# Building a row table batch by batch on three engines, with x in the accumulator and the bias in the matrix multiply

## The chip, the cores and the metric

The kernel runs on one core of one Trainium2 chip. The metric is the device time of that core in microseconds (us), the median of three runs. Engines are named as in the profile: PE (TensorE matmul, with PEld for its weight loads), DVE (VectorE), ACT (ScalarE), POOL (GpSimd) and SP (SyncE, which here only issues DMAs).

## The reference

A relational graph layer and then a mixture of experts, both added to x, on 3125 nodes of 256 numbers, 53125 edges (sorted by dst) of 8 relations:

```python
h_all = einsum('ni,roi->rno', layernorm(x), weight)       # 8 relations
messages = segment_sum(h_all[edge_types, src], dst, 3125)
x = x + messages + bias
# then, on layernorm(x): 16 experts of width 512, the best 2 for each node,
# x = x + sum over the two of gate * (silu(n @ w1) * (n @ w2)) @ w3
```

## The kernel before

**Head.** The nodes are 25 tiles of 125 rows, and x comes in five loads of five tiles (`LOAD`, `X_LOADS`). From x the kernel makes a table in HBM, `x_tab`: each normalized row, scaled, is kept as two f16 numbers per element, a high part and a low part (the rest). The stages for this are:

- SP queues three loads of edges (dst, type, src), the ten pieces of x (L386, two for each load), three small tensors, the last of them `gb_sb`, and the relation weights `w_raw`.
- DVE casts the edges (L771 to L773), takes the least and the greatest dst of each chunk of 125 edges (L775, L776), and takes bn_stats of each x tile as its load lands (L782). Only when all 25 are there does it combine them (L784 to L790), for all tiles at once; ACT takes one square root (L594), DVE one reciprocal (L803).
- Then, tile by tile, DVE normalizes (`normalize`, L812) into a ring `xn` of six places, ACT casts to the high part (L600), and DVE subtracts for the low part (L824). For the last five tiles POOL subtracts (L492). SP stores five tiles at a time into `x_tab` (L400).
- POOL, ahead of this, waits for the last x load and for the small tensors, and then adds x and the bias, broadcast to all partitions, into the accumulator `acc` with one instruction over all 25 tiles (L485).
- PE transposes the edge rows and the chunk ends (L1212, L1214) into PSUM, and three eighths of the weights (L1221).
- After the last low part DVE reads the transposed keys (L828) and chunk ends (L830), and works out from them, in some twenty small steps on one partition, the places at which sums are added (L834 to L860). PE spreads a line of them over the partitions (L1228), DVE ends that part at L870 (`edges_done`), and ACT and DVE finish the weights (L610, L877).

**Sweep.** 25 turns follow, one for each node tile. In a turn POOL gathers 17 chunks of 125 rows of `x_tab` (L501, one indirect DMA for each chunk) into `got`, DVE makes one-hot matrices (L882), PE multiplies them in six groups (L1244, `window`), and DVE adds each group into `store` (L900) and then copies that group's indices for the next turn (L902). It is this copy that lets POOL gather the same group of the next turn. The first copy for turn 1 comes after the first add. At the end of a turn ACT takes the sums as a high part (L636) and DVE as a low part (L912), and PE multiplies both with the relation weights in 48 matmuls (L1256, `messages`). DVE adds the result to `acc` (L921), and takes the statistics of the second layernorm. PE's order in turn i is: windows 3, 4, 5 of tile i, transpose, window 0 of tile i+1, gate logits, messages of tile i-1, windows 1 and 2 of tile i+1.

**After the sweep** come routing, the expert loop and the combination of each node's two expert rows with `acc`.

The edges here allow one single sweep; a general form with many sweeps is in the same loops (`tiles_n`, `wins_n`), and its registers are read from counts at run time.

Of the kernel before, what the change touches and what calls it, by code (L numbers as in the profile page):

```python
# [29 lines left out]
I32 = mybir.dt.int32  # L30
ALU = mybir.AluOpType
# [15 lines left out]
POOL_ROWS = LOAD  # L47
# [43 lines left out]
def build(nc, x, src, dst, etype, w_rel, b_rel, gate_w, gate_b, w1, w2, w3, out):  # L91
# [5 lines left out]
    with ExitStack() as ctx:  # L97
# [58 lines left out]
        single_i = sb("single_i", [1, 1], I32)  # L156
        n_tiles = sb("n_tiles", [1, 1], I32)
# [101 lines left out]
        edges_turned = sem("edges_turned")  # L259
        first_ready = sem("first_ready")  # L260
# [11 lines left out]
        pool_low = sem("pool_low")  # L272
# [36 lines left out]
        choice_begun = sem("choice_begun")  # L309
# [14 lines left out]
        half_begun = sem("half_begun")  # L324
# [11 lines left out]
        xs_drained = sem("xs_drained")  # L336
# [34 lines left out]

        def node_tile(i, b, single):
# [6 lines left out]
        def _(sp):  # L379
            for hbm, rows in ((dst, e_dst), (etype, e_typ), (src, e_src)):  # L380
                sp.dma_start(rows, hbm.rearrange("(q e) -> q e", q=EQ)).then_inc(edges_in, 16)
            for n in range(X_LOADS):
                t0, t1 = n * LOAD, (n + 1) * LOAD
                rows = x[t0 * TP:t1 * TP, :].rearrange("(t p) d -> p t d", p=TP)
                for p0, p1 in SPREAD:
                    sp.dma_start(x_sb[p0:p1, t0:t1, :], rows[p0:p1, :, :]).then_inc(x_in[n], 16)  # L386
            sp.dma_start(bias[:, :], b_rel.rearrange("(a d) -> a d", a=1).to_broadcast([P, DIM])).then_inc(small_in, 16)
            sp.dma_start(gw_sb[:, :, :], gate_w.rearrange("(k p) e -> p k e", p=P)).then_inc(small_in, 16)
            sp.dma_start(gb_sb[:, :], gate_b.rearrange("(a d) -> a d", a=1).to_broadcast([P, EXPERTS])).then_inc(small_in, 16)
            sp.dma_start(w_raw, w_rel.rearrange("r (a p) i -> p (r a) i", p=P)).then_inc(w_in, 16)  # L390

            for n in range(X_LOADS):
                sp.wait_ge(row_high, (n + 1) * LOAD)
                sp.wait_ge(row_low, min((n + 1) * LOAD, TILES - POOL_ROWS))
                if (n + 1) * LOAD > TILES - POOL_ROWS:
                    sp.wait_ge(pool_low, (n + 1) * LOAD - (TILES - POOL_ROWS))
# [28 lines left out]
            for n in range(X_LOADS):  # L425
                t0, t1 = n * LOAD, (n + 1) * LOAD
                sp.wait_ge(x2_kept, before + (t1 + 1))
                sp.sem_inc(half_begun, 1)
# [7 lines left out]
            def store_oct(q):  # L436
                for n in range(2):
                    sp.wait_ge(oct_got[n], (q + 1) * HALF_OCT * 16)
                    sp.sem_inc(half_begun, 1)
# [3 lines left out]
                    sp.sem_inc(half_begun, 1)  # L443
# [24 lines left out]
        def _(pool):  # L468
# [12 lines left out]
            nc.gpsimd.memset(logit[:, :, :], 0.0).then_inc(acc_init, 1)  # L481
            for n in range(X_LOADS):
                pool.wait_ge(x_in[n], 2 * 16)
            pool.wait_ge(small_in, 48)
# [4 lines left out]
            for t in range(TILES - POOL_ROWS, TILES):  # L489
                pool.wait_ge(row_high, t + 1)  # L490
                row = got[0:TP, t % (3 * LOAD), :]
                nc.gpsimd.tensor_tensor(row[:, DIM:], xn[0:TP, t % XN, :], row[:, 0:DIM], ALU.subtract).then_inc(pool_low, 1)  # L492
# [95 lines left out]
        def _(act):  # L588
# [849 lines left out]
```

## Time and profile before

| | |
|---|---|
| median of three runs | 1097.66 us (1096.2 to 1099.3) |
| time of the profiled execution | 1098.44 us |
| its span, first to last instruction | 1096.7 us |
| busy: PE, POOL, DVE, ACT | 761.1, 730.0, 613.2, 331.7 us |
| granted PE clock, mean share of full speed | 0.828 |

The profile is of one execution. Busy time is a sum over the span, and says little of which engine sets the end of a stage. The time of the profiled execution is that of the same run from outside, 1.7 us more than its span. In a row of a timeline the first number is the start, the second how long the instruction, or the merged run of `xN` instructions, took; in brackets stands how long the engine sat idle before, and what ended that.

### The profile page before, as it was taken

To read this page: it belongs to the slowest core of one execution; us is meant where nothing else is said; L and a number is where in the kernel's file an instruction comes from. 1 tells how busy PE (TensorE), PEld (TensorE's weight loads), DVE (VectorE), ACT (ScalarE), POOL (GpSimd) and SP (SyncE) were. 2 spreads that over 40 slices of the span, in tenths; PEclk is the share of its full clock that TensorE was granted. 3 is DMA by queue.
4 is the path that set the end of the run, shared out by engine and by line. 5 is a ranking of instruction groups with operands and counts; after the bars stand their busy time and mean duration, and the time that the engine had idled before them with its cause. 6 is when DMAs were issued, how large, how long until landed. Compare 5 with 4: busy or idle time off the path is not lost.

```text
span 1096.7 us, 18853 instructions
## 1 busy us (share of the span) xinstructions
PE 761.1 (69%) x4904; PEld 651.1 (59%) x4905; DVE 613.2 (56%) x1431; ACT 331.7 (30%) x368; POOL 730.0 (67%) x627
## 2 busy tenths in 40 slices
PE   1137668767688767887767863289999899997600
PEld 1024557756577655676656752278887788886500
DVE  5975575656746566665665767854443334433433
ACT  0332333335433344333453343122322223221100
POOL 2467777777777777777777720667363777767476
PEclk9656887988877898788887886599999989998855
DMA  9253454444544333433334314077355357555346
GB/s 212 75 184 100 135 159 133 129 129 129 158 120 122 96 96 100 119 96 100 97 96 121 95 41 139 29 230 239 115 177 172 97 189 236 161 191 112 91 125 179
DMA packets 93628, 145.97 MB, mean 133 GB/s; under 512 B 13367, under 2 KB 67595, under 8 KB 93610
## 3 DMA queue, kind: packets, MB, share of 16 engines
q0 software_dynamic: 25968, 70.94, 23.2%
q1 hardware_dynamic: 50794, 59.48, 17.2%
q10 hardware_dynamic: 16848, 15.34, 4.5%
q8 instruction: 7, 0.11, 0.0%
q14 instruction: 11, 0.09, 0.0%
HBM read 109.90 MB, written 33.98 MB: 131 GB/s over the span
## 4 chain that ended last, share of the span: by engine, by line
PE 37%; issue 17%; DMA 14%; POOL 13%; DVE 9%; ACT 4%; DVEq 3%; SPq 1%; ACTq 1%; POOLq 0%
PE ps L1256 12%; PE ps L1378 9%; POOL got L501 7%; PE ps L1244 7%; PE ps L1360 6%; DMA got<-x_tab,idx 5%; DMA y_tab<-ffn 5%; ACT part L636 3%; POOL x_sb L571 2%; POOL store L582 2%; PE ps L1386 1%; DMA xs_tab<-x_sb 1%; DVE store L900 1%; DVE mean L784 1%; DVEq L900 1%
## 5 line engine op out<-in xcount | busy, mean ns | idle before, releaser
L501 POOL DMA_INDIRECT got<-x_tab,idx x425 | 446.5, 1051 | 134.3 <-issue 112.7
L1244 PE MATMUL ps<-hot,got 125*128 125x256 f16 x1700 | 252.3, 312 | 140.2 <-DMA got<-x_tab,idx 126.1
L1244 PEld LDWEIGHTS ps<-hot,got 125*128 125x128 f16 x1700 | 178.8, 110 | 202.1 <-issue 139.6
L1378 PE MATMUL ps<-part,operands 128*128 x696 | 177.9, 405 | 1.2 <-DVE operands L1133 1.2
L900 DVE TENSOR_TENSOR store<-store,ps 128x512 f32 x150 | 102.7, 685 | 136.0 <-PE ps L1244 126.9
L1256 PE MATMUL ps<-part 128*128 128x256 f32 x1152 | 166.7, 312 | 1.0 <-DVE part L912 0.8
L1256 PEld LDWEIGHTS ps<-part 128*128 128x128 f32 x1152 | 163.0, 221 | 1.6 <-DVE part L912 1.3
L1378 PEld LDWEIGHTS ps<-part,operands 128*128 128x128 f32 x696 | 129.3, 192 | 27.0 <-issue 2.0
L912 DVE SCALAR_TENSOR_TENSOR part<-store,part 128x1024 fp32r<-128x1024 f32 x48 | 94.8, 2019 | 64.9 <-ACT part L636 64.9
L882 DVE TENSOR_SCALAR hot<-key_row,pass,drel 125x256 f16<-125x256 f16 x425 | 126.2, 367 | 5.7 <-issue 5.1
L1360 PE MATMUL ps<-part,operands 128*128 x696 | 101.7, 296 | 24.3 <-DVE operands L1143 24.1
L636 ACT ACTIVATE part<-store 128x2048 fp32r x24 | 93.8, 3906 | 48.8 <-DVE store L900 48.8
L1360 PEld LDWEIGHTS ps<-part,operands 128*128 128x128 f32 x696 | 90.1, 195 | 30.1 <-issue 28.2
L621 ACT ACTIVATE dev<-mv,eps 125x1 f32<-125x1 f32 x25 | 7.4, 295 | 317.5 <-DVE mv L927 317.5
L524 POOL TENSOR_TENSOR part<-store,part 128x2048 fp32r<-128x2048 f32 (+1 forms) x28 | 97.9, 3496 | 2.3
L1143 DVE TENSOR_TENSOR operands<-ps,operands 128x512 fp32r<-128x512 f32 x58 | 40.1, 691 | 95.5 <-ACT operands L701 95.5
L701 ACT CAST operands<-ps 128x512 fp32r<-128x512 f32 x58 | 34.1, 587 | 181.7 <-issue 90.0
L522 POOL TENSOR_SCALAR part<-store 128x2048 fp32r<-128x2048 f32 (+1 forms) x28 | 41.6, 1486 | 70.6 <-PE ps L1378 58.3
L535 POOL DMA_INDIRECT x_sb<-x_tab,oct_idx x64 | 61.0, 954 | 23.4 <-issue 16.2
L1139 DVE COPY ffn<-ps 128x256 f32<-128x256 f32 x58 | 24.6, 425 | 66.9 <-PE ps L1360 43.3
L1153 DVE TENSOR_TENSOR ffn<-ffn,ps 128x512 f32<-128x512 f32 x58 | 39.7, 685 | 32.5 <-PE ps L1378 25.5
L643 ACT COPY store<-store x25 | 56.2, 2246 | 0.0
(200 smaller groups left out, 700.6 us busy)
## 6 DMA issues: line engine op xcount, KB each, us to landing
store<-in_L_ffn_w SPq DMA_DIRECT2D x48, 512.0 KB, 5.8
xs_tab<-x_sb SPq DMA_DIRECT2D x16, 512.0 KB, 3.5
y_tab<-ffn SPq DMA_DIRECT2D x9, 896.0 KB
ffn<-xs_tab ACTq DMA_DIRECT2D x59, 128.0 KB, 2.2
y_tab<-ffn ACTq DMA_DIRECT2D x58, 128.0 KB
got<-x_tab,idx POOLq DMA_INDIRECT x425, 2.8
x_sb<-in_x SPq DMA_DIRECT2D x5, 560.0 KB
x_tab<-got SPq DMA_DIRECT2D x5, 560.0 KB
```

What stands on the lines that cost most here:

```text
L501: nc.gpsimd.indirect_dma_start(got[:, c, :], None, x_tab, bass.IndirectOffsetOnAxis(ap=idx[:, c:c + 1], axis=0)).then_inc(gathered[c], 16)
L524: nc.gpsimd.tensor_tensor(part[:, 2 * k + 1, at:at + cols], whole, high.bitcast(F32), ALU.subtract).then_inc(done, 1)
L535: nc.gpsimd.indirect_dma_start(xg[:, u, :], None, x2_tab, bass.IndirectOffsetOnAxis(ap=oct_idx[:, u:u + 1], axis=0)).then_inc(oct_got[u // ...
L636: nc.scalar.activation(high, buffer(v, 0, P * RELS).rearrange("p k (n r) -> p k r n", r=RELS), ACT.Copy, scale=1.0 / SCALE).then_inc(tile_ ...
L643: nc.scalar.copy(buffer(v + 1, 0, BK - TK), buffer(v, TK, BK)).then_inc(moved_on, 1)
L882: v.tensor_scalar(hot[0:CE, g % HOT, c - GROUPS[g][0], :], key_row[0:CE, :], pass0[0:CE, 0:1], drel[0:CE, bass.ds(turn * TC + c, 1)], ALU. ...
L900: v.tensor_tensor(window, window, ps[:, WIN_BANK[g], :].rearrange("p (k n) -> p k n", k=KT), ALU.add).then_inc(win_added, 1)
L912: last = v.scalar_tensor_tensor(out=low[:, k, :, :], in0=whole_sums, scalar=1.0 / SCALE, in1=high[:, k, :, :].bitcast(F32), op0=ALU.mult, ...
L1244: last = mm(ps[:, WIN_BANK[g], k * KEYS:(k + 1) * KEYS], got[0:CE, c, a * DIM + k * P:a * DIM + (k + 1) * P], hot[0:CE, g % HOT, c - c0, : ...
L1256: last = mm(ps[:, bank, 0:DIM], (high, low)[a][:, k, r, :], wT[:, b, k, r * DIM:(r + 1) * DIM], start=(r == 0 and k == 0 and a + b == 0), ...
L1360: last = mm(ps[:, Y_BANK, 0:DIM], hidT[:, a, k, :], part3[:, bass.ds(at + b, 1), k, :].rearrange("p a n -> p (a n)"), start=(k == 0 and a ...
L1378: last = mm(ps[:, UP_BANK + w, :], xsT[:, a, k, :], part12[:, bass.ds(at + b, 1), w, k, :].rearrange("p a n -> p (a n)"), start=(k == 0 an ...
```

## The change

- **Loads.** x goes straight into `acc`. SP issues loads 0, 2 and 4, ACT issues 1 and 3. The bias is one row of 1 KB and stands beside a row of zeros (`bias[1, 2, DIM]`).
- **Statistics.** For each load DVE takes bn_stats and then bn_aggr tile by tile, ACT one square root, DVE one reciprocal (`statistics`, `spread_x`).
- **Rows.** POOL normalizes all 25 tiles, ACT casts, DVE subtracts all 25 (`low_rows`). DVE's order is statistics of batch n, then low rows of batch n-1; ACT's is the root of batch n+1, then the casts of batch n.
- **Edges.** The least and greatest dst of the chunks are taken after the last low row. Their ten transposes move in PE's order behind the first three eighths of the weights and have a semaphore of their own (`ends_turned`), which DVE awaits behind the copy of the keys.
- **Bias.** POOL's large add is gone. `messages` starts with one f32 matmul, a column of ones against one row of `bias`: the bias at a tile's first visit, the zeros at any later one. PE chooses the row by a register.
- Some semaphores of no effect on the order are merged (`half_begun`, `choice_begun`, `xs_drained`).

```diff
@@ sync
-            for n in range(X_LOADS):
...
-                    sp.dma_start(x_sb[p0:p1, t0:t1, :], rows[p0:p1, :, :]).then_inc(x_in[n], 16)
-            sp.dma_start(bias[:, :], b_rel.rearrange("(a d) -> a d", a=1).to_broadcast([P, DIM])).then_inc(small_in, 16)
+            for n in range(0, X_LOADS, 2):
                 for p0, p1 in SPREAD:
+                    sp.dma_start(acc[p0:p1, n * LOAD:(n + 1) * LOAD, :], x_rows(n)[p0:p1, :, :]).then_inc(x_in[n], 16)
...
+            sp.dma_start(bias[:, 0, :], b_rel.rearrange("(a d) -> a d", a=1)).then_inc(small_in, 16)
...
-                sp.wait_ge(row_high, (n + 1) * LOAD)
-                sp.wait_ge(row_low, min((n + 1) * LOAD, TILES - POOL_ROWS))
...
+                sp.wait_ge(row_low, (n + 1) * LOAD)
@@ gpsimd
-            nc.gpsimd.tensor_tensor(acc[:, :, :], x_sb[0:TP, :, :], bc(bias[0:TP, :], [TP, TILES, DIM], 1),
-                                    ALU.add).then_inc(acc_init, 1)
...
+            pool.wait_ge(iota_used, 1)
+            for t in range(TILES):
+                if t % LOAD == 0:
+                    pool.wait_ge(rstd_done, t // LOAD + 1)
+                if t >= XN:
+                    pool.wait_ge(row_low, t - XN + 1)
+                nc.gpsimd.tensor_scalar(xn[0:TP, t % XN, :], acc[:, t, :], mv[0:TP, t, 0:1], rstd[0:TP, t:t + 1],
+                                        ALU.subtract, ALU.mult).then_inc(xn_ready, 1)
@@ scalar
+            for n in range(1, X_LOADS, 2):
+                for p0, p1 in SPREAD:
+                    act.dma_start(acc[p0:p1, n * LOAD:(n + 1) * LOAD, :], x_rows(n)[p0:p1, :, :]).then_inc(x_in[n], 16)
...
+            def spread_x(n):
+                t0, t1 = n * LOAD, (n + 1) * LOAD
+                act.wait_ge(stats_done, t1)
+                nc.scalar.activation(dev[0:TP, t0:t1], mv[0:TP, t0:t1, 1], ACT.Sqrt, bias=eps[0:TP, 1:2], scale=SCALE ** -2).then_inc(dev_done, 1)
+            spread_x(0)
             for t in range(TILES):
+                if t % LOAD == 0 and t + LOAD < TILES:
+                    spread_x(t // LOAD + 1)
                 act.wait_ge(xn_ready, t + 1)
...
@@ vector
+            v.tensor_copy(src_f, e_src).then_inc(edge_rows, 1)
+            def statistics(n):
+                t0, t1 = n * LOAD, (n + 1) * LOAD
+                dve.wait_ge(x_in[n], 2 * 16)
+                for t in range(t0, t1):
+                    v.bn_stats(stat[0:TP, t, :], acc[:, t, :]).then_inc(stats_raw, 1)
+                for t in range(t0, t1):
+                    dve.wait_ge(stats_raw, t + 1)
+                    v.bn_aggr(mv[0:TP, t, :], stat[0:TP, t, :]).then_inc(stats_done, 1)
+                dve.wait_ge(dev_done, n + 1)
+                v.reciprocal(rstd[0:TP, t0:t1], dev[0:TP, t0:t1]).then_inc(rstd_done, 1)
+            def low_rows(n):
+                for t in range(n * LOAD, (n + 1) * LOAD):
+                    dve.wait_ge(row_high, t + 1)
+                    row = got[0:TP, t % (3 * LOAD), :]
+                    v.tensor_tensor(row[:, DIM:], xn[0:TP, t % XN, :], row[:, 0:DIM], ALU.subtract).then_inc(row_low, 1)
+            statistics(0)
+            for n in range(1, X_LOADS):
+                statistics(n)
+                low_rows(n - 1)
...
+            low_rows(X_LOADS - 1)
             by_chunk = dst_f.rearrange("p (j e) -> p j e", j=EJ)
             v.tensor_reduce(ends[:, 0, :], by_chunk, AX.X, ALU.min)
+            v.tensor_reduce(ends[:, 1, :], by_chunk, AX.X, ALU.max).then_inc(ends_ready, 1)
...
+            dve.wait_ge(ends_turned, 1)
@@ tensor
+            pe.wait_ge(ends_ready, 1)
+            for j in range(EJ):
+                for n in range(2):
+                    last = nc.tensor.transpose(ps[0:1, 2 + n, j * EQ:(j + 1) * EQ], ends[:, n, j:j + 1], ident[0:EQ, 0:EQ])
+            last.then_inc(ends_turned, 1)
...
+            def messages(v0, i, w, bank=MSG_BANK, high=tileT[:, 0, :, :, :], low=tileT[:, 1, :, :, :]):
+                n = v0 + i
+                pe.reg_alu(bias_row, pe.snap((w + i) * several, min_val=0), 1, ALU.min)
                 pe.wait_ge(tile_low, n + 2)
                 if bank == MSG_BANK:
                     pe.wait_ge(acc_added, n + 1)
+                which = pe.snap(bias_row, min_val=0, max_val=1)
+                mm(ps[:, bank, 0:DIM], ones[0:1, :], bias[0:1, bass.ds(which, 1), :].rearrange("p a d -> p (a d)"), start=True, stop=False)
```

## Rows read from the trace of the kernel before

**Rows 1.** Page, part 5 (groups of instructions): POOL's gathers.

```profile
L501 POOL DMA_INDIRECT got<-x_tab,idx x425 | 446.5, 1051 | 134.3 <-issue 112.7
```

**Rows 2.** Waits of POOL, 84 to 640 us: in total, times, longest.

```profile
POOL got L501 <- issue: 103.0, 338, 0.3
...
POOL got L501 <- DVE idx L902: 21.6, 71, 0.3
```

**Rows 3.** Timeline of POOL: start, duration, instruction, [idle before].

```profile
25.59 13.68 POOL L485 TENSOR_TENSOR acc<-x_sb,bias 125x6400 f32<-125x6400 f32 x1 [20.89 <-DMA gb_sb<-in_L_ffn_gate_b]
...
54.93 3.69 POOL L492 TENSOR_TENSOR got<-hot,got 125x256 f16<-125x256 f32 x5 [15.66 <-ACT got L600]
...
63.73 1.23 POOL L501 DMA_INDIRECT got<-x_tab,idx  x1 [5.11 <-issue]
...
85.36 0.95 POOL L501 DMA_INDIRECT got<-x_tab,idx  x1 [0.30 <-DVE idx L902]
...
638.50 0.94 POOL L501 DMA_INDIRECT got<-x_tab,idx  x1 [0.30 <-issue]
```

**Rows 4.** Timeline of DVE, 0 to 84 us.

```profile
13.09 0.79 DVE L776 TENSOR_REDUCE ends<-store 85x5 f32<-85x625 f32 x1
...
13.86 1.73 DVE L782 BATCH_NORM_STATS2 stat<-x_sb 125x6 f32<-125x256 f32 x5
...
24.83 1.73 DVE L782 BATCH_NORM_STATS2 stat<-x_sb 125x6 f32<-125x256 f32 x5 [1.19 <-DMA x_sb<-in_x]
...
26.60 12.73 DVE L784 TENSOR_TENSOR mean<-stat 125x25 f32<-125x25 f32 x1
...
58.65 0.92 DVE L828 COPY key_c<-ps 125x425 f32<-125x425 f32 x1 [1.22 <-POOL got L492]
...
59.61 1.84 DVE L830 COPY store<-ps 1x425 f32<-1x425 f32 x2
...
83.32 0.41 DVE L902 COPY idx<-gidx 125x3 int32<-125x3 int32 x1
```

**Rows 5.** Windows view: stretch, busy us by engine, PEclk, DMA share, GB/s.

```profile
8.00:10.00 2.00, 0.00 (x0) 0.00 (x0) 0.00 (x0) 0.00 (x0) 0.00 (x0) 1.00 1.11 236
...
64.00:79.00 15.00, 6.31 (x22) 4.42 (x22) 9.76 (x29) 5.63 (x7) 11.37 (x12) 0.50 0.64 219
```

**Rows 6.** Timelines of ACT and DVE: single operations that the change multiplies.

```profile
40.11 0.32 ACT L594 ACTIVATE dev<-var,eps 125x25 f32<-125x25 f32 x1 [37.71 <-DVE var L790]
...
43.26 0.41 ACT L600 CAST got<-hot 125x256 f16<-125x256 f32 x1 [0.25 <-DVE hot L812]
...
54.99 0.42 DVE L824 TENSOR_TENSOR got<-hot,got 125x256 f16<-125x256 f32 x1
...
593.24 0.18 DVE L927 BATCH_NORM_AGGREGATE mv<-stat 125x2 f32<-125x6 f32 x1 [0.15 <-DVE stat L924]
```

**Rows 7.** Groups of POOL by form: the two tensor_scalar sizes.

```profile
L522 POOL TENSOR_SCALAR part<-store 128x2048 fp32r<-128x2048 f32 x14 | 26.8, 1918 | 68.8 <-PE ps L1378 58.3 <-DMA store<-in_L_ffn_w 10.3
...
L522 POOL TENSOR_SCALAR part<-store 128x1024 fp32r<-128x1024 f32 x14 | 14.8, 1055 | 1.7 <-PE ps L1360 1.7
```

**Rows 8.** Timeline of PE, 0 to 90 us.

```profile
14.02 0.69 PE L1212 MATMUL ps<-ident,store 85*125 85x85 f32 x2 [14.02 <-DVE ends L776]
...
17.31 0.49 PE L1214 MATMUL ps<-ident,ends 85*1 85x85 f32 x2
...
65.54 1.78 PE L1228 MATMUL ps<-store,ones 1*128 1x426 f32 x2 [31.77 <-DVE store L849]
...
79.39 8.93 PE L1244 MATMUL ps<-hot,got 125*128 125x256 f16 x68 [5.20 <-DVE hot L882]
```

**Rows 9.** Timelines of PE and DVE around one turn.

```profile
582.11 6.80 PE L1256 MATMUL ps<-part 128*128 128x256 f32 x48
...
602.86 8.19 PE L1256 MATMUL ps<-part 128*128 128x256 f32 x48 [0.41 <-DVE part L912]
...
598.86 3.95 DVE L912 SCALAR_TENSOR_TENSOR part<-store,part 128x1024 fp32r<-128x1024 f32 x2 [2.70 <-ACT part L636]
```

More of the change, by code:

```diff
@@ L480, in _ @@
             nc.gpsimd.memset(ffn[:, :], 0.0).then_inc(zeros_set, 1)
[L481 to L484, printed above, removed]
[L485 to L492 removed]
+            nc.gpsimd.memset(logit[:, :, :], 0.0).then_inc(rows_zeroed, 1)
+            nc.gpsimd.memset(bias[:, 1, :], 0.0).then_inc(rows_zeroed, 1)
+            pool.wait_ge(iota_used, 1)
[6 more added lines that the diff above has]
+                                        ALU.subtract, ALU.mult).then_inc(xn_ready, 1)
             def gather_turn(n):
@@ L774, in _ @@
+            low_rows(X_LOADS - 1)
             by_chunk = dst_f.rearrange("p (j e) -> p j e", j=EJ)
             v.tensor_reduce(ends[:, 0, :], by_chunk, AX.X, ALU.min)
-            v.tensor_reduce(ends[:, 1, :], by_chunk, AX.X, ALU.max).then_inc(edge_rows, 1)
-            for n in range(X_LOADS):
-                dve.wait_ge(x_in[n], 2 * 16)
-                for t in range(n * LOAD, (n + 1) * LOAD):
-                    v.bn_stats(stat[0:TP, t, :], x_sb[0:TP, t, :]).then_inc(stats_raw, 1)
-            dve.wait_ge(stats_raw, TILES)
@@ L784, in _ @@
-            v.tensor_tensor(mean[0:TP, :], stat[0:TP, :, 1], stat[0:TP, :, 4], ALU.add)
-            v.tensor_tensor(var[0:TP, :], stat[0:TP, :, 2], stat[0:TP, :, 5], ALU.add)
-            step(v.tensor_tensor(dev[0:TP, :], stat[0:TP, :, 1], stat[0:TP, :, 4], ALU.subtract))
-            v.tensor_scalar(mean[0:TP, :], mean[0:TP, :], 0.5, None, ALU.mult)
-            step(v.scalar_tensor_tensor(out=dev[0:TP, :], in0=dev[0:TP, :], scalar=0.25, in1=dev[0:TP, :],
-                                        op0=ALU.mult, op1=ALU.mult))
@@ L856, in _ @@
                                    op0=ALU.mult, op1=ALU.add).then_inc(counts_ready, 1)
+            v.tensor_scalar(several_i[:, :], even[:, :], -1.0, 1.0, ALU.mult, ALU.add)
             v.tensor_copy(single_i[:, :], even[:, :]).then_inc(counts_ready, 1)
@@ L1211, in _ @@
                 for bank, rows in ((0, src_f), (1, key_f)):
-                    nc.tensor.transpose(ps[0:CE, bank, out_cols], rows[:, j * CE:(j + 1) * CE], ident[0:EQ, 0:EQ])
-                for n in range(2):
-                    last = nc.tensor.transpose(ps[0:1, 2 + n, out_cols], ends[:, n, j:j + 1], ident[0:EQ, 0:EQ])
+                    last = nc.tensor.transpose(ps[0:CE, bank, out_cols], rows[:, j * CE:(j + 1) * CE], ident[0:EQ, 0:EQ])
             last.then_inc(edges_turned, 1)
@@ L1284, in _ @@
             wins_n = pe.value_load(n_wins[0:1, 0:1], min_val=1, max_val=GEN_W)
+            several = pe.value_load(several_i[0:1, 0:1], min_val=0, max_val=1)
+            pe.wait_ge(small_in, 48)
+            pe.wait_ge(rows_zeroed, 2)
             with pe.Fori(0, tiles_n) as b:
```

89 lines of the change are left out of this document (30 added, 59 removed).

## The prediction

> **What bounds the kernel now.** I read the page first, then the waits of POOL, then the timelines of the first 90 us. The page's largest group is POOL's gather: 425 of them, 446.5 us busy and 134.3 us idle before them, of which 112.7 are a fixed 0.3 us of issue each [rows 1]. In the waits of 84 to 640 us no single wait of POOL lasts over 0.3 us, and the one on DVE's index copy, 71 times, is no longer than the ordinary issue [rows 2]. So in the sweep POOL is never kept waiting: it issues from 63.73 to 638.50 without a gap [rows 3], (638.50 - 63.73) / 424 = 1.356 us for each gather, 23.05 us for a turn of 17. A gather by itself takes 0.95 + 0.30 = 1.25, which makes 21.25 a turn; the missing 1.8 us are gathers that stretch beside L912. **The sweep is a rigid block on POOL. What the head saves or loses is what its first gather, or a gather soon after it, moves.**
>
> The head before: x lands in five loads, the first by 13.86, the last at 24.83 [rows 4]. Then DVE's first two-input operation, 25 numbers wide, takes 12.73 us, from 26.60 to 39.33. A bn_aggr on as little data takes 0.18 [rows 6]. It ends with POOL's add over all tiles, 25.59 + 13.68 = 39.27 [rows 3]: DVE was shut out by it. The last low row is done at 54.93 + 3.69 = 58.62; call this time T. The first gather starts at T + 5.1, after the last table store. On DVE the chain of small steps starts at T too, and ends in the first index copy, at 83.32 + 0.41 = 83.7 = T + 25.1. The eighteenth gather, the first that needs this copy, starts at 85.36 = T + 26.7. So only 1.6 us of slack lie between the DVE chain and POOL's stream.
>
> **The change, step by step.** First T itself.
>
> 1. *First load.* The loads are (24.83 - 13.86) / 4 = 2.74 us apart, with the DMA engines' share already at 1.11 [rows 4, 5]: transfers set the pace, not their issue. ACT now queues loads 1 and 3 at once, beside SP's edges and load 0. If they share the engines, load 0 waits for both: 13.86 + 2 x 2.74 = 19.3. The edges come later too, by 0 to 5.5, with 1.7 us of casts behind them; that is under this wait. Bounds for this step: 13.9 (load 0 undisturbed) and 19.3. I take the late end, since the engines are full. (The Trainium skill, DMA: Bandwidth & Descriptors, section "Issuing engines are not separate DMA queues", says that transfers from several issuing engines interleave on the same sixteen DMA engines, and that spreading saves only issue time. The share in the trace agrees. It speaks against this edit: by it the last load lands no earlier and the first one later. Were it wrong, the second queue would add bandwidth, and the sum below would be 5.5 us smaller, 1083.7.)
> 2. *Statistics of a batch.* Five bn_stats 1.73 [rows 4], five bn_aggr at up to 0.18 alone [rows 6], overlapped about 0.12, so 0.6: 2.3 us. ACT's root 0.32 [rows 6] and two hand-overs of 0.1: 0.5. Reciprocal 0.2. POOL starts on batch 0 at 19.3 + 3.0 = 22.3.
> 3. *A POOL row.* No tensor_scalar of 256 columns with pointer scalars is in the trace. From 2048 and 1024 columns the slope is (1918 - 1055) / 1024 = 0.84 ns a column, the rest 0.19 us, so 0.41 us a row [rows 7]. Above it stands the two-input 3.69 / 5 = 0.74 [rows 3]. I take 0.41, as the rows are of the same operation; five are 2.1 us, which fit beside DVE's next statistics.
> 4. *Low rows of a batch.* ACT casts batch n-1 only after the root of batch n: first cast 0.4 us [rows 6]. DVE then subtracts five times. Alone one takes 0.42, starting every 0.33; POOL is then at batch n, whose rows each wait for a place in the ring that a low row frees. Bounds for a low row: 0.33 and 0.42 + 0.41 = 0.83 if they exclude each other. In the five rows where POOL and DVE alternated before, POOL kept its own pace. I take 0.5, so 2.5 a batch.
> 5. *Sum for T.* 22.3 + 2.8 (statistics 1 and root) + 0.4 + 2.5 + 1.2 (the index casts that stand here once, the first like L828's 0.92) = 29.2. Three cycles of 2.8 + 0.4 + 2.5 = 5.7 make 46.3; five last low rows, with nothing beside them, 1.8. T = 48.1, against 58.6: **-10.5 us**. This is near the 12.5 us for which DVE was shut out; that is the gain, and batching gives back in late load and hand-overs most of what it overlaps.
>
> Now what follows T.
>
> 6. *Table store to first gather.* One store after the last low row as before, T + 5.1: moves with T.
> 7. *Chunk ends.* The two reductions, 0.79 each and slightly overlapped [rows 4], come after T: 1.5 us. Then ten transposes: twenty took 17.31 + 0.49 - 14.02 = 3.8 us [rows 8], so 1.9, and 0.2 for hand-overs: ready at T + 3.6. The key copy (0.92) runs under them. Before, the copies of the ends began at 59.61 = T + 1.0. The chain is 2.6 us longer, 0.1 more for `several_i`, and the index copy comes at T + 27.8, where POOL would want it at T + 26.7: **+1.0 us** of stall, at the first gather of turn 1. Groups behind it have slack: POOL takes 3.8 us for three gathers, DVE's copies come each 1.4.
> 8. *Bias matmul.* The nearest row is the f32 matmul of one row of 426 columns at 1.78 us [rows 8], at a granted clock of 0.50 [rows 5], that is at 1.2 of 2.4 GHz: 1.78 x 256 / 426 = 1.07 at that clock, 0.53 at full. It stands between L912 and the 48 matmuls, on PE's own loop. That loop, from messages to messages without a wait for a gather, is 602.86 - 582.11 = 20.75 us [rows 9] in a turn of 23.05. So 2.3 us a turn cover it, and **0.5** is my allowance for turns in which messages take 8.2 in place of 6.8 us. Without cover it would be 24 x 0.5 to 1.1, 13 to 26 us. At the end of the sweep, with no gathers left, one of the last two is bare: **+0.5**.
> 9. *At nothing:* the x loads' issue on ACT (ACT has nothing to do until the first root), the bias row's load (it is needed 50 us later), PE's extra register load, which runs while PE waits for one-hots until 79.39 [rows 8], the merged semaphores, and the removed add itself, in whose time POOL was idle but for DVE's being shut out. Without their cover the first would cost some 5 us (two loads' share of the issue of five), the register load 0.5, the bias load one short DMA.
>
> Sum: -10.5 + 1.0 + 0.5 + 0.5 = **-8.5 us**. The profiled execution took 1098.44 us, 1.7 more than its span, which I leave alone: 1089.9. It lay 0.8 above the median of the runs, so I predict **1089.2**.
>
> **Rivals.**
> - *POOL and DVE exclude each other in the low rows.* For it: L784. Against: five POOL rows in 3.69 us with DVE working between. At 0.83 a low row four batches take 4 x 1.65 = 6.6 us longer: 1095.8. (The Trainium skill, SBUF — State Buffer, section "Who interferes with whom", has a DVE instruction with two SBUF inputs and a GpSimd instruction that reads SBUF block each other fully. L784 against L485 agrees. By it this would be the likely case, but it tells only that they take turns, not how long POOL's turn is in a short instruction.) Chance 0.12.
> - *Load 0 is not held up,* since SP's entries are ahead in time: T 5.5 earlier, 1083.7. Against: edges and load 0 need the engines long after ACT's first issue. Chance 0.13.
> - *PE becomes the bound of the sweep: slower.* The place is the start of `messages`. If matmul, register work and the waits around it cost more than 2.3 us a turn, all above that is paid 24 times. At 2.8 it is 24 x 0.5 = 12 in place of the 0.5 allowed: 1100.7. The point from which the kernel is slower than before is 2.3 + 9.0 / 24 = 2.7 us. Against: two such matmuls' row says 0.5 to 1.1. Chance 0.06.
> - *The gathers' beat against L912 changes.* 1.8 us are lost each turn there, more or less by phase, and every phase is new: about 0.1 us a turn, +-2.4. This widens the range, with no side.
>
> **How the numbers follow.** The forecast case (a gain of 5 to 12 us) has 0.63, and 1086 to 1093 as its own range; 0.06 are left for what I don't see, half of it on either side of no gain. The 8-in-10 range takes in the second rival and most of the first: 1083 to 1095. A difference of 0.3%, 3.3 us, is about what a measurement of this kernel can tell. Faster by more: 0.63 + 0.13 + a third of the first rival + 0.02 = 0.82. Within it: 0.11. Slower: 0.07.
>
> **What the next profile would show.** Load 0's bn_stats at about 19 and not 14 (step 1); no DVE operation of 12 us; POOL rows of about 0.41 (step 3); cycles of 5.7 us (4); the last low row at 48 (5); first gather 5.1 behind it (6); at the first gather of turn 1 a wait of about 1 us on the index copy (7); one f32 matmul before each `messages`, POOL still without waits until the last gather, and (last - first) / 424 still 1.35 (8). Wrong would make it: POOL rows well above 0.5, which count 25 times in the ring; a wait of POOL on DVE in each turn; or a first gather that no longer follows T by 5.1.

## The result and the profile after

| | before | after |
|---|---|---|
| median of the runs | 1096.93 us (1094.58 to 1099.3) | 1112.78 us (1111.38 to 1115.73) |
| ratio, 95% interval | 1 | 1.0148 (1.0117 to 1.0179) |
| span of the profiled execution | 1096.7 us | 1109.7 us |
| granted PE clock, mean | 0.828 | 0.825 |

Slower by 15.9 us where 8.5 less were forecast. The two spans differ by 13.0 us. I cut both at three events of POOL: the first gather, the last gather, and the first large operation behind the sweep (`x_sb<-got,tile`, L540 before, L535 after).

| | before | after | difference | forecast |
|---|---|---|---|---|
| start to first gather | 63.73 | 59.39 | -4.3 | -10.5 |
| first to last gather (the sweep) | 574.77 | 589.84 | +15.1 | +1.5 |
| last gather to POOL's large operation | 47.88 | 54.39 | +6.5 | +0.5 |
| from there to the end | 410.32 | 406.08 | -4.2 | 0 |

**The head.** Timeline of POOL after, beside [rows 3]:

```profile
21.95 31.48 POOL L486 TENSOR_SCALAR hot<-acc,mv,rstd 125x256 f32<-125x256 f32 x25 [16.83 <-DVE rstd L790]
59.39 1.17 POOL L496 DMA_INDIRECT got<-x_tab,idx  x1 [5.96 <-issue]
...
82.58 0.95 POOL L496 DMA_INDIRECT got<-x_tab,idx  x1 [1.90 <-DVE idx L890]
```

The 25 rows run without a gap, 31.48 us in all, one each 1.26 us, where 0.41 was forecast. A row takes 1.22 us by itself and up to 1.65 where three of DVE's low rows fall into it. Everything else in the head keeps up with them. Timelines of DVE and ACT, beside [rows 4, 6]:

```profile
17.77 1.73 DVE L785 BATCH_NORM_STATS2 stat<-acc 125x6 f32<-125x256 f32 x5 [3.32 <-DMA acc<-in_x]
21.56 0.19 DVE L790 RECIPROCAL rstd<-dev 125x5 f32<-125x5 f32 x1 [1.71 <-ACT dev L597]
...
52.70 0.43 DVE L796 TENSOR_TENSOR got<-hot,got 125x256 f16<-125x256 f32 x1 [0.78 <-ACT got L606]
53.90 0.42 DVE L796 TENSOR_TENSOR got<-hot,got 125x256 f16<-125x256 f32 x1 [0.78 <-ACT got L606]
...
57.48 1.83 DVE L817 COPY store<-ps 1x425 f32<-1x425 f32 x2 [0.91 <-PE ps L1216]
```

```profile
19.93 1.28 ACT L597 ACT_TABLE_LOAD   x1 [19.93 <-DVE mv L788]
21.23 0.30 ACT L597 ACTIVATE dev<-mv,eps 125x5 f32<-125x5 f32 x1
```

DVE waits 0.78 us for each low row. T, the end of the last one, is 53.90 + 0.42 = 54.3. The first gather is 5.06 behind it.

**The sweep.** Waits of POOL, 84 to 649 us, beside [rows 2]:

```profile
POOL got L496 <- issue: 99.7, 327, 0.3
POOL got L496 <- DVE idx L890: 33.8, 79, 1.1
```

POOL now waits for DVE's index copy for up to 1.1 us, which it never did before. The starts of every seventeenth gather give the length of the 24 full turns, 0 to 23: turns 0 to 7 take 21.4 to 23.8 us, and **each of turns 8 to 23 takes 23.87 to 23.92**. Something with a fixed beat of 23.89 has taken over from POOL, whose mean was 23.05. The groups of POOL and PE on the page after show which, beside [rows 1]:

```profile
L496 POOL DMA_INDIRECT got<-x_tab,idx x425 | 450.2, 1059 | 146.5 <-issue 110.8
L1236 PE MATMUL ps<-hot,got 125*128 125x256 f16 x1700 | 204.6, 281 | 32.4 <-DVE hot L870 16.4
...
L1254 PE MATMUL ps<-part 128*128 128x256 f32 x1152 | 205.9, 359 | 0.0
```

The same two groups of PE before:

```profile
L1244 PE MATMUL ps<-hot,got 125*128 125x256 f16 x1700 | 252.3, 312 | 140.2 <-DMA got<-x_tab,idx 126.1
...
L1256 PE MATMUL ps<-part 128*128 128x256 f32 x1152 | 166.7, 312 | 1.0 <-DVE part L912 0.8
```

The windows of PE hardly wait for gathers any more: 32.4 us idle before them in all, against 140.2. The messages, 166.7 us busy and 312 ns each before, take 205.9 and 359. The profile's chain of the work that ended last says the same: in its stretch from 300 to 600 us it holds 76.6 us of POOL's gathers and their DMAs before, and none after. One turn of the timelines of PE, DVE and ACT, beside [rows 9]:

```profile
520.82 8.63 PE L1254 MATMUL ps<-part 128*128 128x256 f32 x48
...
536.92 1.47 PE L1236 MATMUL ps<-hot,got 125*128 125x256 f16 x12 [0.52 <-DVE hot L870]
541.95 1.02 PE L1275 MATMUL ps<-gw_sb,x2T 128*125 128x16 f32 x4 [3.56 <-ACT x2T L635]
543.58 1.21 PE L1250 MATMUL ps<-bias,ones 1*128 x2 [0.61 <-DVE part L900]
544.72 8.62 PE L1254 MATMUL ps<-part 128*128 128x256 f32 x48
```

```profile
534.33 0.69 DVE L888 TENSOR_TENSOR store<-store,ps 128x512 f32 x1 [0.50 <-issue]
...
539.38 3.96 DVE L900 SCALAR_TENSOR_TENSOR part<-store,part 128x1024 fp32r<-128x1024 f32 x2 [2.71 <-ACT part L641]
```

```profile
535.26 3.92 ACT L641 ACTIVATE part<-store 128x2048 fp32r x1 [1.10 <-DVE store L888]
539.08 2.25 ACT L648 COPY store<-store  x1
541.23 0.41 ACT L632 COPY x_sb<-xn 125x256 f32 x1
```

The chain of waits is closed in itself: the last window's sum (L888) frees ACT's split (L641), that frees DVE's (L900), then come the bias matmul, the 48 matmuls, and the windows that stand behind them in PE's order. This is the loop of step 8; I call it PE's ring from here on (it has nothing to do with the ring `xn`). The granted clock in the same turn (windows view; busy us of PE, PEld, DVE, ACT, POOL, then PEclk):

```profile
536.00:538.50 2.50, 1.86 (x14) 1.26 (x14) 0.68 (x3) 2.50 (x1) 1.93 (x2) 1.00 0.36 105
538.50:542.00 3.50, 0.05 (x1) 0.05 (x1) 2.62 (x2) 3.50 (x5) 3.15 (x2) 0.78 0.25 75
542.00:544.70 2.70, 2.09 (x6) 1.36 (x6) 2.70 (x7) 1.66 (x1) 1.81 (x2) 0.50 0.19 49
544.70:549.00 4.30, 4.30 (x21) 4.28 (x21) 4.30 (x17) 0.00 (x0) 3.20 (x4) 0.50 0.31 91
550.00:553.00 3.00, 3.00 (x24) 3.00 (x24) 0.00 (x0) 0.00 (x0) 2.39 (x3) 0.88 0.36 105
553.00:555.00 2.00, 2.00 (x20) 1.78 (x20) 0.00 (x0) 0.00 (x0) 1.39 (x3) 1.00 0.34 105
```

PE stands idle for 3.56 us before the gate logits. In that gap the grant falls from 1.00 to 0.50 of 2.4 GHz, and the bias matmul and the first 6 us of the messages run at 1.2 GHz; the grant is 1.00 again only at 550.8. So messages take 8.6 us, where [rows 9] show 6.80 in the turn from which I took the loop.

That gives a theory in numbers. The loop was 20.75 with messages at 6.80; at the lower clock it is 20.75 + 1.8 = 22.6, still under POOL's 23.05, by 0.5. The bias matmul adds 1.21 and its hand-over 0.1: 23.9, over it. The rows bear this out part by part. One more is needed from DVE's timeline before:

```profile
593.81 0.69 DVE L900 TENSOR_TENSOR store<-store,ps 128x512 f32 x1 [0.38 <-issue]
```

| part of the ring | before, 582.11 to 602.86 | after, 520.82 to 544.72 |
|---|---|---|
| start of the messages to the last window's sum | 11.70 | 13.51 |
| from there to the end of DVE's split | 9.00 | 9.01 |
| end of DVE's split to the next messages | 0.05 | 1.38 |
| sum | 20.75 | 23.90 |

1.8 of the 3.15 us come from the slower messages, 1.3 from the bias matmul.

### The profile page after: what moved, and what is told of

The parts are those of the page before. It is cut to its first block, busy times and chain, and to the rows that moved or that the text cites. A ratio compares the mean times of both kernels' runs of the same rounds, so it can differ in the third digit from the quotient of the medians.

```text
span 1109.7 us, 19013 instructions
## 1 busy us (share of the span) xinstructions
PE 791.8 (71%) x4954; PEld 685.0 (62%) x4955; DVE 595.1 (54%) x1435; ACT 331.8 (30%) x372; POOL 748.0 (67%) x647
## 4 chain that ended last, share of the span: by engine, by line
PE 42%; issue 16%; DVE 11%; POOL 10%; ACT 8%; DMA 8%; DVEq 3%; ACTq 1%; POOLq 0%; SPq 0%
PE ps L1254 17%; PE ps L1379 10%; ACT part L641 8%; PE ps L1361 6%; DVE part L900 4%; PE ps L1236 4%; DMA y_tab<-ffn 3%; POOL hot L486 3%; PE ps L1250 2%; POOL x_sb L566 2%; DVE store L888 2%; POOL store L577 2%; PE ps L1387 2%; DMA acc<-in_x 1%; POOL got L496 1%
## 5 line engine op out<-in xcount | busy, mean ns | idle before, releaser
L1236 PE MATMUL ps<-hot,got 125*128 125x256 f16 x1700 | 204.6, 281 | 32.4 <-DVE hot L870 16.4
L1254 PEld LDWEIGHTS ps<-part 128*128 128x128 f32 x1152 | 201.0, 270 | 15.6 <-issue 15.6
L1254 PE MATMUL ps<-part 128*128 128x256 f32 x1152 | 205.9, 359 | 0.0
L1236 PEld LDWEIGHTS ps<-hot,got 125*128 125x128 f16 x1700 | 166.6, 100 | 63.4 <-issue 34.9
L888 DVE TENSOR_TENSOR store<-store,ps 128x512 f32 x150 | 103.1, 687 | 158.9 <-PE ps L1236 146.3
L900 DVE SCALAR_TENSOR_TENSOR part<-store,part 128x1024 fp32r<-128x1024 f32 x48 | 94.8, 2019 | 66.0 <-ACT part L641 66.0
L870 DVE TENSOR_SCALAR hot<-key_row,pass,drel 125x256 f16<-125x256 f16 x425 | 123.1, 357 | 4.8 <-issue 4.8
L641 ACT ACTIVATE part<-store 128x2048 fp32r x24 | 93.9, 3912 | 50.6 <-DVE store L888 50.6
L1275 PE MATMUL ps<-gw_sb,x2T 128*125 128x16 f32 x100 | 24.7, 366 | 78.6 <-ACT x2T L635 78.6
L1275 PEld LDWEIGHTS ps<-gw_sb,x2T 128*125 128x125 f32 x100 | 22.1, 310 | 85.7 <-ACT x2T L635 85.7
```

Of the source, the lines that this page charges most:

```text
L641: nc.scalar.activation(high, buffer(v, 0, P * RELS).rearrange("p k (n r) -> p k r n", r=RELS), ACT.Copy, scale=1.0 / SCALE).then_inc(tile_ ...
L870: v.tensor_scalar(hot[0:CE, g % HOT, c - GROUPS[g][0], :], key_row[0:CE, :], pass0[0:CE, 0:1], drel[0:CE, bass.ds(turn * TC + c, 1)], ALU. ...
L888: v.tensor_tensor(window, window, ps[:, WIN_BANK[g], :].rearrange("p (k n) -> p k n", k=KT), ALU.add).then_inc(win_added, 1)
L900: last = v.scalar_tensor_tensor(out=low[:, k, :, :], in0=whole_sums, scalar=1.0 / SCALE, in1=high[:, k, :, :].bitcast(F32), op0=ALU.mult, ...
L1236: last = mm(ps[:, WIN_BANK[g], k * KEYS:(k + 1) * KEYS], got[0:CE, c, a * DIM + k * P:a * DIM + (k + 1) * P], hot[0:CE, g % HOT, c - c0, : ...
L1254: last = mm(ps[:, bank, 0:DIM], (high, low)[a][:, k, r, :], wT[:, b, k, r * DIM:(r + 1) * DIM], start=False, stop=(r == RELS - 1 and k == ...
```

## The experiments

Twelve kernels. Unless said otherwise a kernel is the one after with the edit shown. The phases are those of the table above, from one profiled execution each; "msgs" is the mean time of the 24 groups of 48 matmuls in us, "ratio" is the time against the kernel before on the same chip, with its 95% interval.

| | first gather | sweep | to POOL's large op. | rest | msgs | ratio |
|---|---|---|---|---|---|---|
| before | 63.7 | 574.8 | 47.9 | 410.3 | 6.95 | 1 |
| after | 59.4 | 589.8 | 54.4 | 406.1 | 8.58 | 1.0148 |
| no_bias_matmul | 60.2 | 572.7 | 50.3 | 399.4 | 6.78 | 0.9892 (0.9863 to 0.9920) |
| before_plus_zero_row | 64.5 | 587.8 | 54.6 | 409.6 | 8.56 | 1.0192 (1.0165 to 1.0219) |
| bias_in_the_gap | 60.3 | 575.4 | 54.3 | 404.8 | 7.85 | 1.0005 (0.9980 to 1.0031) |
| rows_with_constants | 57.3 | 587.9 | 54.4 | 399.6 | 8.22 | 1.0020 (0.9997 to 1.0043) |
| gap_filled | 60.5 | 576.7 | 50.2 | 403.9 | 6.18 | 0.9978 (0.9951 to 1.0006) |
| bias_f16_pair | 58.3 | 575.6 | 50.4 | 406.1 | 7.84 | 0.9993 (0.9970 to 1.0017) |
| rows_mult_add | 51.6 | 588.2 | 54.4 | 397.7 | 8.52 | 0.9973 (0.9952 to 0.9993) |
| split_rows_early_bias | 54.2 | 577.1 | 54.0 | 406.6 | 7.89 | 0.9964 (0.9951 to 0.9978) |
| all_three_small | 49.5 | 573.5 | 53.0 | 406.8 | 7.85 | 0.9915 (0.9890 to 0.9941) |
| all_three_and_filler | 50.3 | 574.4 | 51.1 | 406.6 | 6.15 | 0.9908 (0.9882 to 0.9934) |
| before_gap_filled | 64.9 | 572.2 | 53.1 | 412.9 | 6.07 | 1.0073 (1.0050 to 1.0096) |

The column "rest" falls into three sets: 409.6 to 412.9 for the three kernels made from before, 403.9 to 406.8 for the seven made from after whose values are the full ones, 397.7 to 399.6 for the three that change values. The last three change the numbers on which the experts are chosen, so some 7 us of their gain need not be the edit's, and I read them by their other columns.

**no_bias_matmul**: without the bias matmul and its register (the bias is left out of the sum; the first of the 48 matmuls now starts it).

```diff
-                which = pe.snap(bias_row, min_val=0, max_val=1)
-                mm(ps[:, bank, 0:DIM], ones[0:1, :], bias[0:1, bass.ds(which, 1), :]..., start=True, stop=False)
```

> The changed kernel without its bias matmul and without the register work before it, so the bias is left out of the result. Theory A (the bias matmul stands on PE's own loop and makes that loop, not POOL, the bound of the sweep): from the first gather to the last, 589.8 us in the changed kernel, comes back to 575 to 578; POOL's wait on the index copy goes from most turns; the time falls from 1112.8 to about 1092 (the head's 4.3 us gain stays). Rival B (the new head or other placement sets the gathers' beat; the matmul is covered): the sweep stays near 590 us and the time near 1111.

Measured: no beat of 23.9, turns of 22.5 to 23.7 from turn 2 on, the sweep 17.2 us shorter than after's and 2.1 shorter than before's. The whole loss in the sweep comes with the bias matmul and its register work, though the matmul is only 1.21 us long; bias_f16_pair, below, keeps the register work and has no beat either.

**before_plus_zero_row**: the kernel before with the same matmul, a row of zeros, in front of its messages.

> The kernel before, with a matmul of a row of zeros at the head of each group of messages, chosen by the same register work; nothing else. Theory A: the sweep goes from 574.8 to about 590 us, turns lock to 23.9 us, the time to 1112 to 1118. Rival B: the sweep stays within 3 us of 574.8, and the time within 4 us of 1097.

```profile
POOL got L505 <- issue: 98.8, 324, 0.3
POOL got L505 <- DVE idx L907: 32.7, 77, 1.1
```

Waits of its POOL: the picture of after, though head and x's path are the old ones. Each turn from 8 to 23 takes 23.84 to 23.98 us, and +13.0 us of sweep and +6.7 behind it follow. The loss doesn't depend on the rest of the change.

**bias_in_the_gap**: the matmul and its waits stand ahead of the gate logits, where PE has its idle gap in the kernel after (and likewise at the end of the sweep).

```diff
                         window(v0, i + 1, 0)
+                        bias_first(v0, i - 1, w)
                         if norm:
                             gate_logits(v0 + i - 2)
```

> The changed kernel with the bias matmul moved ahead of the gate logits, where PE sits idle for 3.6 us in each turn. Theory A1 (the matmul's own 1.2 to 1.5 us on the loop is what costs): a turn falls from 23.9 to at most 22.9, POOL is the bound again, and the time is 1092 to 1096. Theory A2 (the larger part is that PE falls to the lower clock in that gap and does all the messages at 1.2 GHz, 8.6 us against 6.9 on average before): the messages still take 8.6 us; the turn is near 22.7 with POOL again ahead, since a small matmul doesn't keep the clock up. If neither holds (B), the time stays at 1111.

```profile
531.00 1.22 PE L1248 MATMUL ps<-bias,ones 1*128 x2
532.15 1.02 PE L1280 MATMUL ps<-gw_sb,x2T 128*125 128x16 f32 x4
533.01 8.02 PE L1259 MATMUL ps<-part 128*128 128x256 f32 x48
```

The same matmul at the same 1.2 us, no longer behind DVE's split: sweep 575.4, no fixed beat, though the messages take 7.85 us on the mean and nearly all begin at a grant of 0.50. It is the place in the ring that costs, not PE's added work. What stays is the stretch behind the last gather, 54.3 as in after; I come back to it.

**gap_filled**: the bias matmul stays, and twelve more f32 matmuls of the identity, whose results nobody uses, go ahead of the gate logits.

```diff
                         window(v0, i + 1, 0)
                         if norm:
+                            pe.wait_ge(acc_added, v0 + i)
+                            for _ in range(12):
+                                mm(ps[:, MSG_BANK, DIM:DIM + P], ident[:, :], ident[:, :], start=True, stop=True)
                             gate_logits(v0 + i - 2)
```

> The changed kernel, the bias matmul at its place, with twelve f32 matmuls of 128 columns (2.7 us, results unused) put into PE's idle gap of 3.6 us ahead of the gate logits. They take nothing off the loop. Theory A2 (PE falls to 1.2 GHz in that gap and does the messages there, 8.6 us): the granted clock at the start of the messages is 1.0 in place of 0.5, the messages take 6.0 to 6.9 us, a turn comes back to about 23.0 with POOL the bound, and the time falls from 1112.8 to 1090 to 1098. Theory A1 (only the bias matmul's own time counts): messages stay at 8.6 and the turn at 23.9 or more, the time at 1112 or above.

Timeline of its PE, and its clock in the windows view:

```profile
530.63 3.04 PE L1305 MATMUL ps<-ident 128*128 128x128 f32 x24
533.51 0.51 PE L1275 MATMUL ps<-gw_sb,x2T 128*125 128x16 f32 x4
533.95 0.69 PE L1250 MATMUL ps<-bias,ones 1*128 x2
534.57 6.01 PE L1254 MATMUL ps<-part 128*128 128x256 f32 x48
```

```profile
532.00:538.00 6.00, 6.00 (x50) 5.64 (x49) 6.00 (x20) 1.10 (x1) 4.78 (x5) 1.00 0.31 87
```

The grant stays at 1.00. The filler costs 3.0 us, and gate logits (1.02 to 0.51), bias (1.21 to 0.69) and messages (8.62 to 6.01) give back 3.6: the kernel is 18 us faster than after with more work in it. The filler was meant to end ahead of L900's end. In the trace it doesn't: in this turn L900 ends at 532.80 and the filler 0.9 us later, and in 20 of the 22 turns that have it the filler ends 0.7 to 3.1 us behind L900, in the other two later still. PE comes late there because POOL is the bound again and the window ahead waits for a gather (2.26 us in this turn). So the run shows that at the higher clock the ring fits under POOL's turn even with the filler; that a ring-bound turn would hide the filler in its gap is argued, not shown.

**bias_f16_pair**: the matmul at its old place, but cheap: the bias as high and low f16 rows, one pass each.

```diff
-                mm(ps[:, bank, 0:DIM], ones[0:1, :], bias[0:1, bass.ds(which, 1), :]..., start=True, stop=False)
+                for part_n in range(2):
+                    mm(ps[:, bank, 0:DIM], ones_h[:, :], bias_h[:, bass.ds(which * ((2 - part_n) * DIM) + part_n * DIM, DIM)], start=(part_n == 0), stop=False)
```

> The changed kernel with the bias as two f16 rows (high and low part), so two one-pass matmuls of 256 columns at the same place in place of one f32 matmul of 1.2 us: about 0.45 us at 1.2 GHz. Both theories of the loop: 0.8 us less than 23.9 leaves 23.1 a turn, just at POOL's own pace of 23.0, so the lock is loose; sweep 575 to 580 us, time 1094 to 1102. If the register work and the waits, not the matmul's passes, make the 1.2 us, the turn stays at 23.7 or more and the time at 1108 or above.

The bias row now comes over ACT's queue, ACT makes its high part and POOL its low part, all ahead of the statistics. The pair takes 0.60 us. By the sum above the ring is 22.6 + 0.6 = 23.2, next to POOL's 23.05. Measured: turns of up to 23.7 but no beat, POOL's longest wait on the index copy 0.3 us again, sweep 575.6. So the point of decision lies between 0.6 and 1.2 us of added matmul, not at the 2.7 of the forecast. The head gained by a side effect. ACT's copy for the high part brings its table loads forward:

```profile
5.39 1.28 ACT L598 ACT_TABLE_LOAD   x1 [5.39 <-DVEq L777]
...
7.11 1.28 ACT L604 ACT_TABLE_LOAD   x1
```

The first reciprocal comes 2.4 us behind the first bn_stats, not 3.8. The three kernels below that use the pair have this too.

**rows_with_constants** and **rows_mult_add**: where do POOL's 1.2 us come from? The first puts constants in place of the per-row mean and rstd and keeps subtract and multiply (the rows aren't normalized); the second multiplies by a constant and adds 0.

```diff
-                nc.gpsimd.tensor_scalar(..., mv[0:TP, t, 0:1], rstd[0:TP, t:t + 1], ALU.subtract, ALU.mult)
+                nc.gpsimd.tensor_scalar(..., 0.0, SCALE, ALU.subtract, ALU.mult)      # rows_with_constants
+                nc.gpsimd.tensor_scalar(..., SCALE, 0.0, ALU.mult, ALU.add)           # rows_mult_add
```

> The changed kernel with POOL's normalization by constants (0 and 2048) in place of each row's own mean and root; all waits stay. Theory P (the two scalars read from SBUF for each partition make POOL's operation slow, 1.21 us): a row takes 0.4 to 0.5 us, the last low row is done 5 to 6 us earlier than at 54.3, and the time falls to about 1107. Rival S (a short f32 operation on POOL costs 1.2 whatever its scalars, or DVE's subtract shuts it out): the row stays at 1.1 to 1.2 us and the time at 1112.

> The changed kernel with POOL's row operation as times 2048 plus 0 (the form of operation of POOL's weight splits) in place of minus 0 times 2048, which took 1.07 us. Theory O (subtract is what POOL is slow at): a row takes 0.4 to 0.5 us, the last low row is done near 49. Rival F (an operation of 256 columns costs POOL 1.07 us whatever it is, the straight line from 1024 and 2048 columns being wrong for short ones): 1.07 stays and the last low row at 52.2. The time is 1096 to 1107 either way, as the sweep may fall into its 23.9 us pattern early or late.

Timeline of POOL in rows_mult_add:

```profile
22.51 5.27 POOL L486 TENSOR_SCALAR hot<-acc 125x256 f32<-125x256 f32 x10 [17.39 <-DVE rstd L790]
```

With constants a row takes 1.07 us, so the pointers are worth 0.15. With multiply and add it takes 0.41 by itself and 0.46 to 0.52, once 0.69, beside DVE's low rows, and T comes down to 46.3. The price hangs on the pair of operations. L522 of [rows 7], from which the 0.41 was extrapolated, multiplies and adds. The head gained 7.8 us over after's, and the sweep's beat of 23.9 came all the same (from turn 9; with constants from turn 10).

**split_rows_early_bias**: DVE normalizes the first two rows of each batch, POOL three; f16 pair, placed in the gap.

> A version meant to beat both: the f16 bias pair moved into PE's gap ahead of the gate logits, and DVE normalizes the first two rows of each batch of five, POOL the other three (3.6 us of POOL for each cycle of DVE of about 5.5). Theory: POOL's 25 x 1.2 us no longer set the head; the last low row is done at 46 to 49 in place of 54.3, the first gather 5 later; the sweep is POOL's at 573 to 576 us; the time is 1080 to 1088. If DVE and POOL hold each other up in the rows, the last low row stays above 51 and the time is 1088 to 1093.

T 49.1, sweep 577.1: the first version with the full values that is faster than both. The last three rows still wait for POOL at 1.2 us each.

**all_three_small** and **all_three_and_filler**: real rows as multiply and add, f16 pair, in the gap; the second with ten filler matmuls ahead of the pair.

```diff
+                dve.wait_ge(rstd_done, n * 2 + 1)
+                v.scalar_tensor_tensor(mv[0:TP, t0:t1, 0], mv[0:TP, t0:t1, 0], -1.0, rstd[0:TP, t0:t1], ALU.mult, ALU.mult).then_inc(rstd_done, 1)
...
-                nc.gpsimd.tensor_scalar(..., mv[0:TP, t, 0:1], rstd[0:TP, t:t + 1], ALU.subtract, ALU.mult)
+                nc.gpsimd.tensor_scalar(..., rstd[0:TP, t:t + 1], mv[0:TP, t, 0:1], ALU.mult, ALU.add)
```

> The kernel after with three edits: the POOL row as x times rstd plus minus mean times rstd (multiply, add, with pointer scalars), one more small DVE operation per batch for the second scalar; the bias as two one-pass f16 rows; and this pair placed ahead of the gate logits. Theory O (the pair of operations sets the row's price, 0.41 to 0.46 with constants): rows 0.45 to 0.6 us with pointers, T about 47, first gather about 52. Theory S (the loop of the PE is the bound only where its turn exceeds 23.1 us): no lock, sweep 573 to 577 as in bias_in_the_gap and bias_f16_pair. Together 1096.6 - 12 to - 7 = about 1085 to 1090. Rival P (a gain at the head is given back, since the turns of the sweep take what the PE and DVE allow): sweep 580 or more and 1093.

> all_three_small plus ten f32 128-column matmuls of ident in the PE's gap ahead of the bias pair and the gate logits. If the clock of the messages matters although the loop is not the bound (PE less behind at the end of the sweep): messages 6.0 to 6.5 us, the stretch from the last gather to the first POOL add 47 to 50 us instead of 52 to 54, time 2 to 5 us below all_three_small, about 1083. If only the lock matters: the same time within 1 us.

Timeline of POOL in all_three_small:

```profile
20.96 6.58 POOL L490 TENSOR_SCALAR hot<-acc,rstd,mv 125x256 f32<-125x256 f32 x10 [13.24 <-DVE mv L799]
29.86 3.73 POOL L490 TENSOR_SCALAR hot<-acc,rstd,mv 125x256 f32<-125x256 f32 x5 [2.31 <-DVE mv L799]
34.48 3.73 POOL L490 TENSOR_SCALAR hot<-acc,rstd,mv 125x256 f32<-125x256 f32 x5 [0.89 <-DVE mv L799]
39.09 4.39 POOL L490 TENSOR_SCALAR hot<-acc,rstd,mv 125x256 f32<-125x256 f32 x5 [0.89 <-DVE mv L799]
```

These are merged runs of five or ten rows. A single row with pointers takes 0.55 us by itself; beside two or three of DVE's low rows it takes 0.97 to 1.22, which happens twice in each batch but the first and lifts the mean to 0.75. POOL waits for DVE between the batches, and T is 44.4, under the 48.1 of the forecast; some 1.3 us of this is ACT's table load, off the path as in bias_f16_pair. 1086.79 us against 1097.84: this is the gain that the change could have had. The filler on top gives nothing that can be told (1085.66, the intervals overlap): messages come down from 7.85 to 6.15 and the stretch behind the last gather by 1.9, but sweep and head are 0.8 or 0.9 longer in that profile.

**before_gap_filled**: the filler of twelve in the kernel before.

> The kernel before with twelve f32 128-column matmuls of ident ahead of the gate logits of each turn. The turn of before is set by POOL (23.05 us on the mean), so that a higher clock of the messages (6.9 to about 6.2 us) buys nothing in the turns: theory S says 1095 to 1098, within 0.3%. If the clock sets the time of before also: 1085 to 1090.

Missed on the bad side: 1105.02 us, 1.0073 times before. Messages did fall from 6.95 to 6.07, and the sweep only from 574.8 to 572.2, as POOL sets it. But the stretch behind the last gather grew by 5.2. I read this as PE, with 3 us more work in each turn, being further behind POOL when the gathers end; no run separates it. The same filler gave 18 us in after and costs 8 here. Another 2.6 us are lost behind POOL's large operation and 1.2 ahead of the first gather, where this kernel has no edit; what makes them is open.

**before_merged_semaphores**: only the merge of the counters, for the 5 us in "rest".

> The kernel before with only the merge of the counters that nothing waits for (the old half_begun, choice_begun and xs_drained now counted in tiles_begun and stats2_begun), which the prediction costed at nothing. Open point: from POOL's large add to the end the three kernels made from before took 409.6 to 412.9 us, the seven made from after with all values kept 403.9 to 406.8, some 5 us less. If the merge makes this: 404 to 407 us there, and a time 0.4% below before. If not (other addresses or another phase): 409 to 413 us and the same time within 0.3%, sweep and head as before. I expect the second.

It ran on another chip, on which the kernel before took 1311.05 us as well; the ratio is 0.9995 (0.9983 to 1.0007). The merge does nothing there. Its profile can't be set against the others' by phases, so that what shortens the rest by some 5 us in the kernels made from after stays open.

## Why the prediction was wrong, step by step

Between the forecast and the spans lie 21.5 us: 6.2 in the head, 13.6 in the sweep, 6.0 behind its last gather, and 4.2 the other way in the rest, for which nothing was forecast.

**Step 8 failed, and it turned the change into a loss.** With the same matmul off the ring (bias_in_the_gap) the time is that of before, 1.0005. The step took "a loop of 20.75 in a turn of 23.05, so 2.3 us cover it". The size of the matmul was nearly right (1.07 forecast at the low clock, 1.21 measured). The slack was wrong: 20.75 came from one turn whose messages took 6.80, while the row of the very next turn showed 8.19. At the low clock the ring is 22.6 and the cover 0.5. I saw the 8.19 and paid it with an allowance of 0.5 us for the whole sweep, as if it only came now and then. It was common: before, the grant in the first microsecond of the messages was under 0.6 in 18 of 24 turns, and messages took 6.00 to 8.50 us as it came back sooner or later. (The turn of the 20.75 wasn't free of waits for gathers either, as step 8 says: PE has two, 1.08 and 2.47 us, but off the ring.) Once the ring sets the turn, PE no longer waits for gathers at scattered places. Before, it has no gap at all ahead of the first 22 groups of gate logits; after, its wait falls into one gap there, 3.56 us from the sixth group on, the grant is 0.50 at the start of all 24 groups of messages, and they take 8.2 to 8.6. no_bias_matmul and before_plus_zero_row show the cost (17 us off, 13 us on in the sweep), gap_filled shows that the clock matters, bias_in_the_gap that the place does. That the beat keeps itself up through the slow clock, once there, is how I read the sixteen equal turns; no run started it or ended it in mid-sweep. The rival "PE becomes the bound" had the place and the mechanism right, but the point of decision at 2.7 us instead of between 0.6 and 1.2.

The "+0.5 at the end of the sweep", also of step 8, was 6.5. It was priced as one bare matmul of 0.5; the stretch depends on how far PE is behind POOL at the last gather, which the sum had at nothing. A sweep bound by the ring gives 54.4 to 54.6, but the ring is not the only cause: bias_in_the_gap and split_rows_early_bias have no beat and 54.3 and 54.0, while no_bias_matmul, gap_filled and bias_f16_pair have 50.2 to 50.4. What sets PE's lag at the end stays open.

**Step 3 was mis-sized: 1.22 for 0.41 us, 1.26 with what DVE adds.** The slope was taken from a multiply-add and used for a subtract-multiply. "The rows are of the same operation" was so by the profile's name only. This moved T from 46 to 54, about 8 us of the forecast gain. Even the upper bound of 0.74, a two-input operation, was too low.

**Right or nearly so.** Step 1: load 0 came at 17.77, late end 19.3 forecast, 13.86 before. Step 2: POOL's first row starts 4.2 us behind the first bn_stats, forecast 3.0; ACT's table load of 1.28 us, done at 1.11 us before, now stands on this path and makes the difference. Step 6: 5.06 for 5.1. Step 7: DVE's copy of the ends at T + 3.15 for 3.6, and a wait of 1.6 us more than the issue for 1.0. Step 5's T of 48.1 was wrong mainly through step 3: with multiply-add rows the runs gave 46.3 and 44.4. The shut-out of DVE by POOL's add is gone, as said.

**The exclusion rival** didn't come as put: after, most low rows took 0.41 to 0.43 us, seven more, up to 0.78. The twentieth to the twenty-fourth each lay wholly inside a row of POOL, which took the 1.22 us that it takes without one. In rows_mult_add, where the two follow each other quickly, the low row's median is 0.61, between the 0.5 taken and the 0.83 of the rival. POOL's rows stretch as well, where several low rows fall into one: 1.22 to 1.65 after, 0.55 to 1.22 in all_three_small. The Trainium skill, SBUF — State Buffer, section "Who interferes with whom", would have them block each other. The runs bear out that both can get longer, but not that one waits for the whole of the other: two operations side by side took less than the sum of both, and single ones cost each other nothing.

## What to carry to other kernels

Take the slack of a loop with each of its parts at its slowest observed duration, above all PE's at the lower granted clock, and ask whether becoming the bound would put its idle time where it lowers the clock for the longest part. Work put on a ring with 0.5 us of slack is paid in every turn once it is longer than the slack; the same matmul ahead of the wait that ends last cost nothing in the sweep here. Price an operation of POOL from a row with the same pair of ALU operations, or bound it far more widely.

## What was new about the hardware

- POOL, tensor_scalar on 125x256 f32, by itself: 1.07 us (constants) or 1.22 (pointers) for subtract and multiply, 0.41 (constants) or 0.55 (pointers) for multiply and add. Beside several two-input operations of DVE the pointer forms took up to 1.65 and 1.22.
- Twelve f32 matmuls ahead of the gate logits, 3.0 us, kept the grant at 1.00 and took the 48 matmuls behind them from 8.62 to 6.01 us; worth 18 us in the kernel that was bound by PE's ring, a loss of 8 in the one bound by POOL.
- Another chip ran the kernel before in 1311.05 us, against 1096 to 1098. In the profile of before_merged_semaphores there, POOL waited for the index copy twice in each turn for 4.4 us or more, and turns took 29.8 us. Waits of POOL, 100 to 700 us:

```profile
POOL got L498 <- DVE idx L899: 187.4, 93, 5.5
```

Its head is as elsewhere (first gather at 64.45 us); the time is in the sweep and behind it. What differs on that chip stays open.
